# Gates of a graph network on one core: order of the head matmuls, of the staging and of the state additions

## The reference

```
hg = einsum('bnf,gf->bng', h3, Wg[:, :F])
qg = einsum('blf,gf->blg', q, Wg[:, F:]) + bg
attn = sigmoid(hg[:, :, None, :] + qg[:, None, :, :])
qi = einsum('bnlf,blf->bnf', attn, q)
alpha = sigmoid(h3 @ Wq[:, :F].T + qi @ Wq[:, F:].T + bq)
hn = alpha * tanh(qi) + (1 - alpha) * h3
```

## Time and profile before

| | |
|---|---|
| median of 3 runs | 823.54 us (823.35 to 824.7) |
| profiled execution, its own time | 824.55 us |
| its span, first to last instruction | 822.7 us |
| granted TensorE clock, mean | 0.998 |
| TensorE busy | 774.9 us (94%) |
| VectorE busy | 603.2 us (73%) |
| GpSimd busy | 514.3 us (63%) |
| ScalarE busy | 423.7 us (52%) |
| sigmoids of both gates, L798 | 192, 187.3 us busy |
| products, L1958 | 96, 217.8 us busy |
| folds on GpSimd, L582 | 94, 222.8 us busy |

### The profile page before, as it was taken

How to read it: one execution, slowest core, us unless ns; L and a number is a source line. 1 busy time by engine, 2 the same in 40 slices (tenths; PEclk the granted TensorE clock), 3 DMA queues, 4 the chain that set the end, 5 groups by cost and what they waited for, 6 DMA issues and landing times.

```text
span 822.7 us, 10528 instructions
## 1 busy us (share of the span) xinstructions
PE 774.9 (94%) x4176; PEld 639.7 (78%) x4180; DVE 603.2 (73%) x660; ACT 423.7 (52%) x505; POOL 514.3 (63%) x219
## 2 busy tenths in 40 slices
PE   7999999999988999988898889999999999998998
PEld 4669986776645699667665558999999999975886
DVE  8966239999999631888999997764696498565462
ACT  6424447677664342766676725434442454253731
POOL 0625609999998273599999955770785177805500
PEclk9999999999999999999999999999999999999999
DMA  9037525345332463360153327556356446250001
GB/s 364 31 81 232 170 81 154 89 142 154 115 116 77 137 231 131 77 179 2 52 205 116 115 78 282 180 193 227 116 163 216 159 154 209 99 230 0 2 1 39
DMA packets 24409, 111.01 MB, mean 135 GB/s; under 512 B 3620, under 2 KB 6180, under 8 KB 23976
## 3 DMA queue, kind: packets, MB, share of 16 engines
q1 hardware_dynamic: 23240, 104.24, 39.2%
q10 hardware_dynamic: 1120, 6.10, 1.9%
HBM read 100.63 MB, written 0.79 MB: 123 GB/s over the span
## 4 chain that ended last, share of the span: by engine, by line
PE 57%; POOL 19%; DVE 18%; ACT 3%; issue 2%; DMA 0%; DVEq 0%; ACTq 0%
PE ps L1076 27%; POOL prod L582 13%; DVE prod L1958 10%; PE ps L1107 5%; PE ps L1042 5%; POOL prod L585 4%; DVE qi_t L1976 3%; PE ps L1589 3%; PE ps L1234 2%; PE ps L1255 2%; POOL w_lo L570 2%; PE ps L1413 1%; PE ps L1650 1%; PE ps L1235 1%; PE ps L1304 1%
## 5 line engine op out<-in xcount | busy, mean ns | idle before, releaser
L570 POOL TENSOR_TENSOR w_lo<-w_raw,w_hi 128x1536 fp32r<-128x1536 f32 x49 | 183.9, 3764 | 141.6 <-ACT w_hi L662 141.5
L582 POOL TENSOR_TENSOR prod<-prod 128x1024 f32<-128x1024 f32 x94 | 222.8, 2392 | 46.0 <-DVE prod L1958 45.8
L798 ACT ACTIVATE prod<-ps 128x1024 f32<-128x1024 f32 x192 | 187.3, 1023 | 73.3 <-PE ps L1366 61.0
L1958 DVE TENSOR_TENSOR prod<-prod,ps 128x2048 f32<-128x2048 f32 x96 | 217.8, 2281 | 5.1 <-ACT prod L798 3.4
L662 ACT ACTIVATE w_hi<-w_raw 128x1536 fp32r<-128x1536 f32 x60 | 88.9, 1487 | 119.6 <-PE ps L1076 108.2
L1366 PE MATMUL ps<-sel_pair,h_and_q 128*128 128x512 f32 x384 | 128.4, 447 | 16.8 <-ACT prod L798 16.5
L1076 PE MATMUL ps<-w_hi,yt_hi 128*128 128x384 f32 x480 | 123.0, 337 | 0.2 <-POOL w_lo L570 0.2
L1076 PE MATMUL ps<-w_hi,yt_lo 128*128 128x384 f32 x480 | 122.0, 335 | 0.0
L1076 PE MATMUL ps<-w_lo,yt_hi 128*128 128x384 f32 x480 | 122.0, 335 | 0.0
L1366 PEld LDWEIGHTS ps<-sel_pair,h_and_q 128*128 128x128 f32 x384 | 67.0, 190 | 52.0 <-ACT prod L798 31.8
L1042 PE MATMUL ps<-w_raw,h_t 128*128 128x384 f32 x312 | 106.8, 486 | 0.0
(11 more groups left out here) (247 smaller groups left out, 1093.1 us busy)
## 6 DMA issues: line engine op xcount, KB each, us to landing
w_raw<-weights SPq DMA_DIRECT2D x105, 768.0 KB, 4.4
wa_in<-weights SPq DMA_DIRECT2D x6, 768.0 KB, 5.9
w_gat<-weights SPq DMA_DIRECT2D x6, 768.0 KB, 8.0
w_query<-weights SPq DMA_DIRECT2D x3, 768.0 KB, 11.7
h_and_q<-stage_hi SPq DMA_DIRECT2D x24, 96.0 KB, 2.1
h_and_q<-stage_lo SPq DMA_DIRECT2D x24, 96.0 KB, 2.2
a_vec<-gat_vectors ACTq DMA_DIRECT2D x1, 2048.0 KB, 9.7
q_t<-queries ACTq DMA_DIRECT2D x1, 1536.0 KB, 10.5
```

The source lines that it names most:

```text
L570: pool.tensor_tensor(Wl[:, j, :], raw_slab(U, 0, j), Wh[:, j, :], ALU.subtract).then_inc(w_lo_by_pool, 1)
L582: pool.tensor_tensor(v[:, :, 0:32], v[:, :, 0:32], v[:, :, 32:64], ALU.add).then_inc(folded_once, 1)
L798: act.activation(slot_view(s)[:, :, 32 * u:32 * u + 32], args.rearrange("p b (n l) -> p (b n) l", l=LH), ACT.Sigmoid).then_inc(sigmoid_rea ...
L1958: TT(slot_view(s), slot_view(s), ps[:, 6, o:o + L].unsqueeze(1).broadcast_to([P, NB, L]), ALU.mult).then_inc(products_ready, 1)
```

## The change

TensorE: the turn of the second tile comes right behind the first 128 head columns; of the 256 other left columns one matmul (k = 0) stands in front of the first arguments, three beside step 0 and two beside step 1. The six matmuls of the right columns move from steps 0 and 1 (three each) to steps 1 and 2 (two and four), the twelve of the second tile from steps 3, 4, 6 and 7 (three each) to 4, 6 and 7 (four each). ScalarE and VectorE stage the left part behind the sigmoids and the product of step 1, and the right part behind those of step 2. VectorE's turned copy and query copy stand between the first low parts. The old state's additions move from VectorE to GpSimd, in front of its folds of gate 2. SyncE's list is the same.

```diff
@@ gpsimd, in front of a gate's folds
+                if i == 1:
+                    for t in range(NT):
+                        pool.wait_ge(h_ready[t], 2 * i + 2)
+                        pool.tensor_tensor(X[:, t, :], X[:, t, :], H[:, t, :], ALU.add).then_inc(state_added, 1)
@@ scalar, behind the copies to first_hi
-                act.wait_ge(heads_ready, 3 * i + 2)
-                act.wait_ge(query_spread[1 if i == 0 else 3], 128)
-                copy(stage_hi[:, P:FH], ps[:, acc, 0:2 * P]).then_inc(staged_hi, 1)
@@ scalar, steps
                     if s == 1:
+                        act.wait_ge(heads_ready, 3 * i + 2)
+                        act.wait_ge(query_spread[1 if i == 0 else 3], 128)
+                        copy(stage_hi[:, P:FH], ps[:, acc, 0:2 * P]).then_inc(staged_hi, 1)
+                    if s == 2:
                         act.wait_ge(heads_ready, 3 * i + 3)
                         copy(stage_hi[:, FH:F], ps[:, acc + 1, 0:FH]).then_inc(staged_hi, 1)
@@ tensor, beside
-                    if s < 2:
-                        if s == 0:
-                            pe.wait_ge(first_lo, 4 * i + 4)
-                        heads(0, 1, 3 * s, 3 * s + 3)
-                    elif s in (3, 4, 6, 7):
-                        if s == 3:
+                    if s == 0:
+                        first_heads(acc, P, FH, 1, 4)
+                    elif s == 1:
+                        first_heads(acc, P, FH, 4, KC)
+                        pe.wait_ge(first_lo, 4 * i + 4)
+                        heads(0, 1, 0, 2)
+                    elif s == 2:
+                        heads(0, 1, 2, KC)
+                    elif s in (4, 6, 7):
+                        if s == 4:
                             pe.wait_ge(turn_kept[1], e + 1)
                             pe.wait_ge(staged_lo, right + 1)
-                        n = (3, 4, 6, 7).index(s)
-                        lower_heads(3 * n, 3 * n + 3)
+                        n = (4, 6, 7).index(s)
+                        lower_heads(4 * n, 4 * n + 4)
@@ tensor, in front of the steps
                 pe.wait_ge(turn_kept[0], e + 1)
-                first_heads(acc + 1, 0, P)
-                first_heads(acc, P, FH)
+                first_heads(acc + 1, 0, P, 0, KC)
                 turn(1, e)
+                first_heads(acc, P, FH, 0, 1)
@@ vector, in front of the steps
-                if i == 1:
-                    for t in range(NT):
-                        dve.wait_ge(h_ready[t], 2 * i + 2)
-                        TT(X[:, t, :], X[:, t, :], H[:, t, :], ALU.add).then_inc(state_added, 1)
-                for b in range(4):
+                def first_low(b):
+
...
-                stage_low(left, stage_lo[:, P:FH], ps[:, acc, 0:2 * P], stage_hi[:, P:FH])
-                keep_turned(2 * i + 1)
...
+                first_low(0)
+                keep_turned(2 * i + 1)
+                first_low(1)
                 first_copy_query()
+                first_low(2)
+                first_low(3)
                 for s in range(STEPS):
                     gate_product(s)
...
                     if s == 1:
+                        stage_low(left, stage_lo[:, P:FH], ps[:, acc, 0:2 * P], stage_hi[:, P:FH])
+                    if s == 2:
                         stage_low(right, stage_lo[:, FH:F], ps[:, acc + 1, 0:FH], stage_hi[:, FH:F])
```

More of the change, by code:

```diff
@@ L1296, in _, with first_heads @@
                 left, right, lower = HEAD_EVENTS[i]
-                def first_heads(bank, c0, c1):
-                    for k in range(KC):
+                def first_heads(bank, c0, c1, k0, k1):
+                    for k in range(k0, k1):
                         if c0 == 0 and k % 2 == 0:
@@ L1305, in first_heads @@
                                        start=(k == 0), stop=(k == KC - 1))
-                    mm.then_inc(heads_ready, 1)
+                    if k1 == KC:
+                        mm.then_inc(heads_ready, 1)
                 def heads(t, h, k0, k1):
```

## The result

The changed kernel takes **831.86 us** in the median of 4 runs (831.57 to 832.33); the kernel before took 823.88 beside it (4 runs, 823.35 to 824.7). The ratio is 1.0094, with an interval of 1.008 to 1.0108. The profiled execution has a span of 829.9 us, 7.2 longer than before.

What follows compares the result with a forecast made beforehand. TensorE carries 57% of the chain; within gates VectorE and GpSimd are full together. Gate 1's lateness 2.4, gate 2's 1.2 and the clock's 2.4 sum to 6.0 us on 823.54, giving 829.5 us, range 823.0 to 832.0.

Steps and rivals of the forecast that it cites:

- The early product: Start of a gate: the first product starts 1.95 us earlier, at 117.5 instead of 119.47 in gate 1.
- The landing: Step 4: left columns land at 129.0, so arguments 4 are 1.66 us late; TensorE stands still 3.7 us or more.
- Three more matmuls between arguments 4 and 8: Steps 4 to 8: 12 instead of 9 head matmuls add 1.94 us, making arguments 8 come 3.60 late.
- The 0.87 in hand between arguments 8 and product 8: Step 8, gate 1: distance 3.67 against a shortest 2.80 leaves 0.87 us slack, so product 8 is 2.73 late.
- the 0.43 counted: Step 13, gate 1: product ends at 159.99, GpSimd takes it at 160.42, so another 0.43 us is in hand.
- The clock: TensorE's clock falls in the wait ahead of arguments 4: 0 to 1.57 us per gate, taken as 1.2, 2.4 in all.
- Gate 1: Gate 1 ends between 2.3 and 2.73 us late, taken as 2.4, plus 1.2 for the clock.
- Gate 2: Gate 2 ends between 0 and 2.54 us late, taken as 1.2, plus 1.2 for the clock.
- the rival in which the clock holds: Both gates: all lateness as forecast but without the clock's price, 827.1 us; chance 0.25.
- GpSimd's additions: Ahead of gate 2: two state additions, about 1.82 us each on GpSimd, fall in its idle time and cost nothing.
- The rival in which the lead is kept: Both gates: left columns land in time or GpSimd's 1.95 us lead outlives VectorE's lateness, 819.6 us; chance 0.11.
- half the lead: Variant of the rival in which the lead is kept: half of it in one gate gives some 821.6 us.

Runs made afterwards that it cites:

- experiment 1: The changed kernel with one semaphore per group of left columns, so steps 4 to 7 each wait only for their own two transfers: 821.26 us.
- experiment 4: The kernel before with only VectorE's low half of the left staging moved behind its second product: 833.99 us.
- experiment 3: The changed kernel with the second tile's 12 lower head matmuls back in steps 3, 4, 6 and 7, three each: 823.77 us.
- experiment 6: The changed kernel with all five remaining left matmuls beside step 0, left staging behind step 0, three right matmuls each beside steps 1 and 2: 823.96 us.
- experiment 2: The changed kernel with 17 extra matmuls of 512 columns, which nobody reads, behind arguments 3: 827.31 us.
- experiment 5: The kernel before with only the old state's two additions moved from VectorE to GpSimd: 823.28 us beside 824.37.
- experiment 9: The changed kernel measured once more, nothing altered: 830.79 us beside 824.22 for the kernel before.

## Why the prediction was right, and where it was short

**The early product** was right: 117.5 forecast, 117.85 - 0.34 = 117.51 measured.

**The landing** was right too: first transfer forecast from 122.5, issued at 122.70; arguments 4 forecast at 129.0, measured 128.98; TensorE idle for 4.25 us where "3.7 us or more" was said. Taken away (experiment 1), it leaves a faster kernel; made alone (experiment 4), it gives a slower one; and with the wait filled (experiment 3) nothing is lost. So the loss is an unfilled wait for the landing, the clock that falls with it, and the work that stands behind it.

**Three more matmuls between arguments 4 and 8** were priced at 1.94, and experiments 3 and 6 differ by 1.94. But against the kernel before the distance at full clock grows by 1.31 only (13.06 against 11.75). With the same nine matmuls experiment 3 needs 11.12, so 0.63 was in hand there, and the forecast had nothing. One wait between the two steps of the kernel before is short but visible:

```profile
131.79 2.02 PE L1413 MATMUL ps<-prod,ident 128*128 128x128 f32 x16 [0.21 <-POOL prod L582]
```

**The 0.87 in hand between arguments 8 and product 8** was wrong. The distance is 3.67 before and 148.34 - 144.68 = 3.66 after, so nothing of it is slack. What stands there is ScalarE's work, in the changed kernel:

```profile
145.18 0.81 ACT L666 ACTIVATE stage_hi<-ps 128x768 fp32r<-128x768 f32 x1 [1.10 <-PE ps L1047]
...
147.69 0.62 ACT L666 ACTIVATE ps<-q_t 128x512 f32<-128x512 f32 x1
```

The first is the staging of the second tile's heads, released by the late head matmuls and in front of the sigmoids of step 8. The second, behind these sigmoids, copies the next queries to PSUM, and product 8 waits for it (the bracket of 0.98 above). Both move with the late steps. The prediction should have asked what the extra time waits for before counting it as slack.

**The two slacks nearly cancelled, and that was luck.** Experiment 2 shows the changed order at full clock, with 0.03 to add for its head (112.14):

```profile
145.67 2.29 DVE L1967 TENSOR_TENSOR prod<-prod,ps 128x2048 f32<-128x2048 f32 x1 [1.01 <-ACT ps L666]
...
199.61 2.29 DVE L1967 TENSOR_TENSOR prod<-prod,ps 128x2048 f32<-128x2048 f32 x1 [0.22 <-ACT prod L799]
```

Product 8 is 2.94 late there, against 2.73 forecast: 0.87 was counted that was not there, and 0.63 was there that was not counted. The slack behind product 8 was larger than the 0.43 counted. The products of step 14, in the kernel before and in the changed one:

```profile
161.79 4.47 DVE L1958 TENSOR_TENSOR prod<-prod,ps 128x2048 f32<-128x2048 f32 x2
```

```profile
166.17 2.28 DVE L1963 TENSOR_TENSOR prod<-prod,ps 128x2048 f32<-128x2048 f32 x1
```

That is 4.04 late (166.17 - 0.34 - 161.79), down from 5.24 at product 8: 1.20 was taken up by step 14. From there on the lateness stays. At the product where the kernel before leaves GpSimd's chain (197.74, here at 202.29) it is 4.21, and at the end of the gate 4.22; in experiment 2 it is 1.90 at that product. The reading of the earlier trace rows, two engines full together that give nothing back, held.

**The clock** is the term that was mis-sized: 1.2 us per gate, with an upper bound of 1.57, where 2.3 and 2.8 were measured (experiment 6 against the changed kernel). The bound was read from the one slow stretch of the kernel before, as if a stretch had one length. It was 3.4 us long there and 6.8 here, in each gate, with 4.9 and 5.9 us on work. The direction was right: the Trainium skill, "TensorE: Matmul & The Clock Gate", section "HAM oscillation — how this bites in real kernels", says that an engine that waits for data between bursts starts each burst at half rate. The trace agrees, with 0.50 behind waits of 4.25 and 4.24 us, and experiment 2 with 1.00 where the same time was filled; the waits of 2.16 and 2.11 in experiment 6's trace had no such fall behind them.

**Gate 1** was forecast at 2.4 + 1.2 = 3.6 and came out at 4.22: 1.9 of lateness and 2.3 for the clock. **Gate 2** was forecast at 1.2 + 1.2 = 2.4 and came out at 2.89. There the kernel before was not undisturbed itself. These are the products right ahead of its slow stretch at 375.7, in the kernel before, in experiment 2 (head at 331.98) and in the changed kernel:

```profile
374.45 2.28 DVE L1958 TENSOR_TENSOR prod<-prod,ps 128x2048 f32<-128x2048 f32 x1
```

```profile
378.85 2.27 DVE L1967 TENSOR_TENSOR prod<-prod,ps 128x2048 f32<-128x2048 f32 x1
```

```profile
383.09 2.27 DVE L1963 TENSOR_TENSOR prod<-prod,ps 128x2048 f32<-128x2048 f32 x1
```

Behind their heads they stand at 45.60, 46.87 and 49.68 us. So the lateness is 1.27, near the 1.2 forecast, and the clock adds 2.81. Of these 4.08 us, 2.89 are left at the end of the gate, because the kernel before pays 1.2 for its own slow stretch. The whole sum is then 1.9 + 1.3 of lateness (3.6 forecast), 2.3 + 2.8 for the clock (2.4 forecast), less 1.2 for the stretch that the kernel before had (nothing forecast): 7.1 us of the spans. The clock's price was off by a factor of two, and the last term hid part of it; that the total came so near the forecast's 6.0 owes something to this. The 827.1 given for the rival in which the clock holds was closer to its case: experiment 2, where it was held, took 827.31.

**GpSimd's additions** were costed at nothing, and experiment 5 shows no cost and a gain of 0.4 us in gate 2. In the changed kernel both are done before the first fold of gate 2, which even waits:

```profile
334.50 1.81 POOL L632 TENSOR_TENSOR x<-x,h 128x768 f32<-128x768 f32 x1 [5.09 <-ACT h L691]
...
341.12 2.38 POOL L582 TENSOR_TENSOR prod<-prod 128x1024 f32<-128x1024 f32 x1 [4.81 <-DVE prod L1963]
```

**The rival in which the lead is kept** did not come true for the change, but its mechanism is real. It named two conditions: columns landed by 125.4, or a lead in GpSimd's queue that outlives VectorE's lateness. In experiment 1 no column lands sooner than in the changed kernel, and each step only stops waiting for the columns of others. The rows there look like the second condition: GpSimd 1.78 ahead, product 8 only 0.24. It took 821.26, near the 821.6 given for half the lead, and 819.34 without a slow stretch.

What stays open: whether GpSimd's queue alone carries the lead of experiment 1 past step 8, and why the single slow stretches of 3.4 us fall where they do.

## What to carry to other kernels

When work is moved behind the first products of a stage, follow it to its last reader through its transfers; if the reader's wait counts a whole set, give each part its own semaphore, which here turned a loss of 8 us into a gain of 2.8. Idle time of TensorE is worth more than its length, since the work behind it can run at half clock; the narrower wait brought 10.6 us here (experiment 1), and filling the wait with matmuls that have to be done anyway brought 8.1 without touching the wait's end (experiment 3). And a distance longer than the shortest one is slack only if what fills it does not hang on the same late work.

## What the hardware showed that was not expected

In the changed kernel's two traces a wait of 4.24 to 4.25 us was followed by a granted clock of 0.50 for 6.8 us in three of four gates and for 3.4 in the fourth (experiment 9's gate 1). In experiment 4 waits of 3.71 and 4.18 us brought 3.4 us each. The fall came inside the wait (127.4 in the changed kernel) or only when the work behind it had begun (experiment 9 and gate 1 of experiment 4). Waits of 2.15, 2.16 and 2.11 us were followed by none. What such a stretch cost was about half of the part that lay on work.

Single stretches of 3.4 us turn up in gates without such a wait too, at different places: in gate 2 of the kernel before at about 375.7, in experiment 1 at 249.7. That one cost 1.2 us there: between the products at 249.75 and 255.47 lie 5.72 us in the kernel before, and between those at 248.70 and 255.65 in experiment 1, 6.95. By the times of whole runs it is more: the kernel before took 822.34 to 822.84 us at a mean granted clock of 1.000 and 823.70 to 824.78 at 0.998, and experiment 1 took 819.34 and 819.35 against 821.26 to 821.71. Two executions of one kernel can differ by 2 us without any edit behind it, a quarter of the effect that was looked for here.
